# Start of a fused attention and mixture kernel: one batch of x loaded and normalised alone, weights behind it, inverse roots on GpSimd, identity products in TensorE's pauses

## The chip, the cores and the metric

One core of one Trainium2 chip runs the whole program in one launch. The metric is the device time of a run in microseconds. Engines are named TensorE (PE, and PEld for its weight loads), VectorE (DVE), ScalarE (ACT), GpSimd (POOL) and SyncE (SP, which issues most loads and stores).

## The reference

Inputs: x of 16 batches x 128 tokens x 256 features, a context of 16 x 128 x 128, and positions of two coordinates per token. All of it is float32.

```python
x = x + xattn(layernorm(x), ctx, pos)      # 32 heads of 8, axial rotation of q and k
x = x + ffn(layernorm(x))                  # shared part + 6 of 32 experts per token

def layernorm(x): return (x - mean(x)) / sqrt(var(x) + 1e-5)

def xattn(x, ctx, pos):
    q = rope(x @ Wq, pos)
    k, v = split(ctx @ Wkv); k = rope(k, pos)
    return softmax(q k^T / sqrt(8)) v @ Wout + bout
```

The second half is a mixture of experts with grouped top-6 routing. The change does not touch it.

## The kernel before, in words

The program has two blocks, `attention` (from line 175) and `mixture` (from line 687). Each writes one instruction stream per engine, with semaphores between them, in an order laid down by hand. A stream runs in program order, so an instruction that waits holds all that stands behind it on its engine. The block of attention ends with all its engines before the mixture begins.

Attention works batch by batch (128 tokens). `periods` (line 242) calls `period(b)` for b = -3 to 17. In period b the kernel works on batch b's exponentials and weighted values, on batch b+1's logits, on batch b+2's keys and on batch b+3's normalised input and projections. Each period has eight slots g. So b = -3 holds only the input of batch 0, b = -2 that of batch 1 with the key transposes of batch 0, and b = -1 has the first logits.

What stands in the start, by engine:

- SyncE issues all loads on one queue, in this order (lines 284 to 292): positions, x batches 0 to 3 (512 KB), the first context (64 KB), WQ, WKV, WO (256 KB each), the broadcast bias BO (128 KB), then x batches 4 to 7, 8 to 11 and 12 to 15. `period` adds the further contexts, the four copies that spread kT into kz (line 305, one batch at a time, after `kT_ok` and `kz_zero`), and the rows of negated maxima (line 312).
- GpSimd fills constants: identities `identf` and `identh` (lines 323 to 328), zeros and ones of `tokst` and `V`. Then it waits for BO and, per batch, adds BO to x once its normalised copy exists (`add_bias`, line 341), and for every batch but the first makes `split` (line 258): the rotated q and k are summed and cut into a high and a low f16 part. In b = -3 it fills both kz with zeros (line 352).
- ScalarE takes the sine (line 361), the square root of variance + epsilon for batches 0 to 3 (`std`, line 363) and, in b = -1, for batches 4 to 15 (line 408). `norm` (line 368) makes xn, the normalised batch, from scale rs1 and bias nb1. `evac_xcT` copies the transposed xn and context out of PSUM, and lines 404 and 420 copy the transposed q (qst) and k (kT).
- VectorE makes the angles, then `statistics(0, 4, 0)` (line 445): four bn_stats, four bn_aggr, plus epsilon, then the rotation tables, the reciprocal of ScalarE's root, and nb1 = -mean * rs1. Per batch it rotates with `rope_cos` (line 475) and `rope_sin` (line 482). It makes the split of batch 0 (line 544). `statistics(4, 16, 1)` (line 546) follows the rotation of batch 1. The maxima of the logits are `row_max` (line 490).
- TensorE waits for WQ, WKV and WO together (line 646). Per batch come `transpose_xc` (line 556), `project_k`, `project_q` (lines 564, 568), then transposes of k and q, `project_v`, `logits_q`, `logits_k`, `weigh_values` and the output steps. `transpose_xc` of a batch waits until the rotation of the batch before has read the bank M1 (`rope_ok`).

## Time and profile before

| what | us |
|---|---|
| runs (three) | 378.28, 380.01, 381.38 |
| median of the runs | 380.01 |
| the profiled execution's own time | 381.89 |
| its span, first to last instruction | 380.1 |
| attention block, from the start | to about 221.6 |
| TensorE, VectorE, ScalarE, GpSimd busy | 323.4, 231.2, 200.1, 153.4 |

The rows below are from one profiled execution. Times count from the start of the span. In a timeline row, the first number is the start, the second the time until the last of the merged instructions ends, and the bracket tells how long the engine stood idle before and what ended that. DVE is VectorE, ACT ScalarE, POOL GpSimd; "q" behind a name is the engine's instruction sequencer, which issues loads. PEclk is the TensorE clock that the throttle granted, as a share of full speed.

### The profile page before, as it was taken

What the parts mean: (1) busy time and instruction counts of PE and PEld (TensorE: products, weight loads), DVE (VectorE), ACT (ScalarE), POOL (GpSimd) and SP (SyncE); (2) the same over time, 40 slices, a digit from 0 to 9 for tenths busy, and PEclk for the clock granted to TensorE, in tenths of its full rate; (3) what the DMA queues carried; (4) which work ended last, traced back from release to release, by engine and by line L of the source; (5) the groups of instructions that cost most, each with busy time, mean ns of one, the idle gap of its engine ahead of it and who ended that gap; (6) DMA issues with size and microseconds to landing.
All of it is one profiled execution on the core that took longest, in us unless ns stands there. A gap on an engine that the chain in (4) does not pass through costs nothing. (4 is left out here: it accounts for less than half of the span.)

```text
span 380.1 us, 9475 instructions
## 1 busy us (share of the span) xinstructions
PE 323.4 (85%) x3094; PEld 218.2 (57%) x3094; DVE 231.2 (61%) x650; ACT 200.1 (53%) x390; POOL 153.4 (40%) x240
## 2 busy tenths in 40 slices
PE   0776998999999999999979738797999989999940
PEld 0455676777777777777656423445574765555520
DVE  4486777767777767777757444588757242544430
ACT  3236766767677776776766457382324341333310
POOL 4555431455324554235400065035498520425560
PEclk9999999999999999999998956999999998999995
DMA  6411113444444454443310013302214174974446
GB/s 173 167 35 37 30 29 111 128 120 109 129 125 122 111 139 109 132 113 100 96 45 0 2 37 130 118 0 44 72 35 148 31 226 119 290 211 50 51 48 221
DMA packets 33293, 37.93 MB, mean 100 GB/s; under 512 B 7808, under 2 KB 27568, under 8 KB 33200
## 3 DMA queue, kind: packets, MB, share of 16 engines
q1 hardware_dynamic: 22610, 22.03, 19.9%
q10 hardware_dynamic: 8030, 11.93, 11.1%
q0 software_dynamic: 2624, 3.61, 5.7%
q8 instruction: 16, 0.26, 0.3%
q14 instruction: 13, 0.11, 0.1%
HBM read 26.36 MB, written 8.96 MB: 93 GB/s over the span
## 5 line engine op out<-in xcount | busy, mean ns | idle before, releaser
L494 DVE TENSOR_REDUCE mx<-bank 128x4 f16<-128x512 f32 x128 | 88.1, 689 | 29.7 <-PE bank L599 28.4
L391 ACT ACTIVATE pw<-bank 128x512 f32<-128x512 f32 x128 | 76.8, 604 | 36.3 <-PE bank L623 21.1
L264 POOL TENSOR_TENSOR rot<-t 128x256 f32<-128x256 f32 x30 | 21.2, 726 | 95.4 <-DVE t L487 95.4
L599 PE MATMUL bank<-kz,qst 128*128 128x512 f16 x128 | 48.8, 382 | 4.0 <-issue 2.9
L612 PE MATMUL bank<-qst,kz 128*128 128x128 f16 x512 | 50.3, 221 | 0.7 <-DMA qst<-mxs 0.7
L612 PEld LDWEIGHTS bank<-qst,kz 128*128 128x128 f16 x512 | 35.8, 98 | 15.2 <-issue 6.7
L623 PE MATMUL bank<-pw,V 128*32 128x128 f32 x1024 | 38.6, 280 | 0.0
L931 POOL DMA_INDIRECT acc<-ac,dst x16 | 23.6, 1472 | 36.9 <-ACT ac L1013 24.7
L623 PEld LDWEIGHTS bank<-pw,V 128*32 128x32 f32 x1024 | 25.4, 110 | 13.5 <-issue 12.6
L1233 PE MATMUL mbank<-hT,WSG 128*128 128x512 f16 (+1 forms) x144 | 32.0, 379 | 0.0
L501 DVE COPY mxs<-bank 8x128 f16<-8x128 f16 x64 | 13.3, 208 | 19.9 <-PE bank L603 19.9
L1233 PEld LDWEIGHTS mbank<-hT,WSG 128*128 128x128 f16 (+1 forms) x144 | 15.1, 106 | 15.5 <-ACT ac L967 0.4
L1245 PE MATMUL mbank<-WSD,ac 128*128 128x256 f32 (+1 forms) x96 | 21.7, 382 | 2.0 <-POOL ac L887 2.0
L887 POOL TENSOR_TENSOR ac<-ac,sg 128x512 f32<-128x512 f32 (+1 forms) x9 | 11.8, 1323 | 25.5 <-ACT ac L967 25.4
L275 POOL TENSOR_TENSOR tokst<-rot,tokst 128x256 f16<-128x256 f32 x30 | 20.2, 673 | 4.4
L1017 ACT ACTIVATE ac<-mbank 128x176 f32<-128x176 f32 x16 | 5.1, 318 | 31.2 <-PE mbank L1323 29.4
L1323 PE MATMUL mbank<-ring_gu,xbT 128*64 128x352 f32 x112 | 20.5, 488 | 0.8 <-ACT xbT L807 0.8
L1245 PEld LDWEIGHTS mbank<-WSD,ac 128*128 128x128 f32 (+1 forms) x96 | 18.0, 190 | 5.5 <-POOL ac L887 3.0
L420 ACT COPY kT<-bank 128x1024 f16<-128x1024 f16 x16 | 16.2, 1011 | 7.8 <-PE bank L584 6.6
L603 PE MATMUL bank<-identh,mx 128*128 128x128 f16 x64 | 14.3, 223 | 5.9 <-DVE mx L494 4.5
L570 PE MATMUL bank<-WQ,xcT 128*128 128x256 f32 x64 | 18.6, 418 | 0.0
L643 PE MATMUL bank<-WO,attnT 128*128 128x256 f32 x64 | 17.5, 398 | 0.5 <-ACT attnT L387 0.5
(189 smaller groups left out, 627.1 us busy)
## 6 DMA issues: line engine op xcount, KB each, us to landing
ring_gu<-in_L_ffn_w_gate_up ACTq DMA_DIRECT2D x20, 352.0 KB
kz<-kT SPq DMA_DIRECT2D x64, 64.0 KB, 2.0
ring_dn<-in_L_ffn_w_down ACTq DMA_DIRECT2D x10, 352.0 KB
ring_gu<-in_L_ffn_w_gate_up SPq DMA_DIRECT2D x8, 352.0 KB
X<-in_x SPq DMA_DIRECT2D x4, 512.0 KB, 7.6
table<-ac SPq DMA_DIRECT2D x8, 256.0 KB, 2.1
acc<-X SPq DMA_DIRECT2D x4, 512.0 KB, 3.1
out<-acc SPq DMA_DIRECT2D x4, 512.0 KB, 5.3
```

The source lines that it names most:

```text
L264: eng.tensor_tensor(rot[:, part], t1[:, part], t2[:, part], ALU.add).then_inc(rot_ok[w], 1)
L275: eng.tensor_tensor(tokst[m.par][:, w, :, a:a + HD], r, hi, ALU.subtract)
L391: act.activation(pw[g % 4][:, :], STB[g % 2][:, :], ACT.Exp, scale=SCALE).then_inc(exp_ok, 1)
L494: dve.tensor_reduce(mx[u // 2 % 2][:, u % 2:8:2], SB[u % 2][:, :].rearrange("p (j t) -> p j t", j=4), axis=AX.X, op=ALU.max, negate=True). ...
L570: ins = pe.matmul(M1[:, 0:D], xcT[m.par][:, c, :], WQ[:, c, :], start=(c == 0), stop=(c == DK - 1))
L599: pe.matmul(SB[u % 2][:, :], qst[m.par][:, u, :], kz[m.par][:, :, u, :], start=True, stop=True).then_inc(s_mm, 1)
L612: ins = pe.matmul(STB[g % 2][:, j * P:j * P + P], kz[m.par][:, j, g, :], qst[m.par][:, g, :], start=True, stop=True)
L623: ins = pe.matmul(OB[m.par][32 * j:32 * j + 32, (g % 4) * P:(g % 4) * P + P], V[m.par][:, a:a + SLOT], pw[g % 4][:, j * P:j * P + P], star ...
L931: pool.indirect_dma_start(acc[:, :], bass.IndirectOffsetOnAxis(ap=dst[0:USED, k:k + 1], axis=0), ys[j][0:USED, :], None, compute_op=ALU.ad ...
L1233: ins = pe.matmul(GU[2 * (i % 2) + w][0:n, :], WSG[:, c, u, w * SHARED + a:w * SHARED + a + n], hT[:, v, c, 512 * k:512 * k + 512], start= ...
L1245: ins = pe.matmul(DN[m % 2][:, 0:D], ac[k % 2][0:n, f, j * P:j * P + P], WSD[0:n, f, :], start=(f == 0), stop=(f == 2))
L1323: ins = pe.matmul(EB[k % 2][lane, 0:2 * INNER], xbT[:, c, e * CAP:e * CAP + LANE], ring.gu[place][:, e % 2, c, :], start=(c == 0), stop=(c ...
```

## The change

- `XPART` cuts x into loads of batch 0 alone, batches 1 to 5, 6 to 10 and 11 to 15. Behind batch 0 and the first context come WKV and WQ; BO and WO go behind all of x.
- TensorE waits for WKV and WQ only, after its first transposes. WO shares the semaphore of BO, which GpSimd's first bias and TensorE's first output projection wait for.
- The statistics are taken for batch 0, for 1 to 3 and for 4 to 15. `factors` (nb1 = -mean * rs1) is a step of its own. That for batches 1 to 3 stands behind the rotation of batch 0.
- rs1 is (variance + epsilon) to the power -0.5, one tensor_tensor on GpSimd (`spread`), where ScalarE took a square root and VectorE a reciprocal.
- GpSimd fills kz after the power for batches 1 to 3 and before it waits for BO. The power for batches 4 to 15 stands in b = -1, ahead of that period's bias and split.
- `keep_warm(n)` issues n f16 products of the identity with 256 columns into the bank OB[1], whose result nobody reads: 30 before the first transposes, 4 behind them, 12 behind project_q of batch 0, 6 behind that of batch 1.

```diff
@@ -35,6 +35,7 @@
 NB, D, DC = 16, 256, 128
 NH, HD = 32, 8
 QUADS, SLOT = NH // 4, 32
+XPART = [0, 1, 6, 11, NB]
 DK = D // P
 MAXROW = 3 * HD
 HALF = SLOT // 2
@@ -206,6 +207,7 @@
         st1 = sb("st1", [P, NB, 6])
         mv1 = sb("mv1", [P, NB, 2])
         rs1 = sb("rs1", [P, NB, 1])
+        power = sb("power", [P, NB])
         nb1 = sb("nb1", [P, NB, 1])
         ang = sb("ang", [P, 2, NB, 2, 2])
         turns = sb("turns", [P, 2, NB, 2, 2])
@@ -222,7 +224,7 @@
         ctx_in_s = [sem(f"ctx_in{i}") for i in range(2)]
         consts, consts2, kz_zero = sem("consts"), sem("consts2"), sem("kz_zero")
         mx_zero = sem("mx_zero")
-        stat1, mv1_ok, std1, rs1_ok = sem("stat1"), sem("mv1_ok"), sem("std1"), sem("rs1_ok")
+        stat1, mv1_ok, rs1_ok = sem("stat1"), sem("mv1_ok"), sem("rs1_ok")
         turn_s, sin_s, rope_tab = sem("turn_s"), sem("sin_s"), sem("rope_tab")
         xn_ok, x_biased = sem("xn_ok"), sem("x_biased")
         xcT_mm, xcT_ok = sem("xcT_mm"), sem("xcT_ok")
@@ -283,13 +285,14 @@
         def _(sp):
             sp.dma_start(POS[:, :, :], pos.rearrange("b p a -> p b a")).then_inc(pos_in, 16)
             for c in range(4):
-                sp.dma_start(X[:, 4 * c:4 * c + 4, :], xr[:, 4 * c:4 * c + 4, :]).then_inc(x_in[c], 16)
+                part = slice(XPART[c], XPART[c + 1])
+                sp.dma_start(X[:, part, :], xr[:, part, :]).then_inc(x_in[c], 16)
                 if c == 0:
                     sp.dma_start(CT[0][:, :], ctx_in[0]).then_inc(ctx_in_s[0], 16)
+                    sp.dma_start(WKV[:, :], wkv).then_inc(w_in, 16)
                     sp.dma_start(WQ[:, :, :], wq.rearrange("(c p) n -> p c n", p=P)).then_inc(w_in, 16)
-                    sp.dma_start(WKV[:, :], wkv).then_inc(w_in, 16)
-                    sp.dma_start(WO[:, :, :], wout.rearrange("(c p) n -> p c n", p=P)).then_inc(w_in, 16)
-                    sp.dma_start(BO[:, :], bout.rearrange("(a n) -> a n", a=1).broadcast_to([P, D])).then_inc(bo_in, 16)
+            sp.dma_start(BO[:, :], bout.rearrange("(a n) -> a n", a=1).broadcast_to([P, D])).then_inc(bo_in, 16)
+            sp.dma_start(WO[:, :, :], wout.rearrange("(c p) n -> p c n", p=P)).then_inc(bo_in, 16)
 
             def period(b):
                 m1, m4 = b + 1, b + 4
@@ -342,14 +345,25 @@
                 at_least(pool, xn_ok, m.n + 1)
                 pool.tensor_tensor(X[:, m.n, :], X[:, m.n, :], BO[:, :], ALU.add).then_inc(x_biased, 1)
 
-            pool.wait_ge(bo_in, 16)
+            pool.memset(power[:, :], -0.5).then_inc(consts, 1)
+            pool.wait_ge(consts, 7)
+
+            def spread(a, e, k):
+                pool.wait_ge(mv1_ok, k + 1)
+                pool.tensor_tensor(rs1[:, a:e, 0], nb1[:, a:e, 0], power[:, a:e], ALU.pow).then_inc(rs1_ok, 1)
+
+            spread(0, 1, 0)
+            spread(1, 4, 1)
+            pool.wait_ge(xn_ok, 1)
+            for i in range(2):
+                pool.memset(kz[i][:, :, :, :].rearrange("p j q t -> p (j q t)").bitcast(F32), 0.0).then_inc(kz_zero, 1)
+            pool.wait_ge(bo_in, 32)
 
             def period(b):
+                if isinstance(b.n, int) and b.n == -1:
+                    spread(4, NB, 2)
                 if inside(b + 3):
                     add_bias(b + 3)
-                    if isinstance(b.n, int) and b.n == -3:
-                        for i in range(2):
-                            pool.memset(kz[i][:, :, :, :].rearrange("p j q t -> p (j q t)").bitcast(F32), 0.0).then_inc(kz_zero, 1)
                     if not (isinstance(b.n, int) and b.n == -3):
                         split(pool, b + 3)
             periods(pool, period)
@@ -360,13 +374,8 @@
             act.wait_ge(turn_s, 5)
             act.activation(ang[:, :, :, :, :], turns[:, :, :, :, :], ACT.Sin, scale=TWO_PI).then_inc(sin_s, 1)
 
-            def std(a, e, k):
-                act.wait_ge(mv1_ok, 2 * k + 2)
-                act.activation(rs1[:, a:e, 0], nb1[:, a:e, 0], ACT.Sqrt).then_inc(std1, 1)
-            std(0, 4, 0)
-
             def norm(m):
-                act.wait_ge(rs1_ok, 2 if isinstance(m.n, int) and m.n < 4 else 4)
+                act.wait_ge(rs1_ok, 6 if not isinstance(m.n, int) or m.n > 3 else 4 if m.n else 2)
                 at_least(act, xcT_mm, m.n)
                 act.activation(xn[:, :], X[:, m.n, :], ACT.Identity, bias=nb1[:, m.n, :],
                                scale=rs1[:, m.n, :]).then_inc(xn_ok, 1)
@@ -391,7 +400,7 @@
                         act.activation(pw[g % 4][:, :], STB[g % 2][:, :], ACT.Exp, scale=SCALE).then_inc(exp_ok, 1)
                     if g == 0 and inside(m1):
                         at_least(act, v_mm, m1.n + 1)
-                        act.wait_ge(consts, 6)
+                        act.wait_ge(consts, 7)
                         at_least(act, pv_mm, QUADS * b.n)
                         act.copy(Vh[m1.par][:, :, :, 0:HD], M0[:, 0:D].rearrange("p (f h d) -> p f h d", f=2, d=HD)).then_inc(v_ok, 1)
                     if g == 0 and inside(m3):
@@ -404,8 +413,6 @@
                             act.copy(qst[m1.par][:, :, :], M0[:, :].bitcast(F16).rearrange("p (q t) -> p q t", q=QUADS)).then_inc(qst_ok, 1)
                     if g == 4 and inside(m4):
                         norm(m4)
-                    if g == 4 and isinstance(b.n, int) and b.n == -1:
-                        std(4, NB, 1)
 
                     if g in (1, 4, 6) and not isinstance(b.n, int):
                         ring.load_first(act, b.n - 2, (1, 4, 6).index(g))
@@ -445,30 +452,30 @@
             def statistics(a, e, k):
 
                 for j in range(a, e):
-                    if j % 4 == 0:
-                        dve.wait_ge(x_in[j // 4], 16)
+                    if j in XPART:
+                        dve.wait_ge(x_in[XPART.index(j)], 16)
                     dve.bn_stats(st1[:, j, :], X[:, j, :]).then_inc(stat1, 1)
                 for j in range(a, e):
-                    dve.wait_ge(stat1, j + 1)
+                    dve.wait_ge(stat1, j + k + 1)
                     ins = dve.bn_aggr(mv1[:, j, :], st1[:, j, :])
-                ins.then_inc(mv1_ok, 1)
-                dve.wait_ge(mv1_ok, 2 * k + 1)
+                ins.then_inc(stat1, 1)
+                dve.wait_ge(stat1, e + k + 1)
                 dve.tensor_scalar(nb1[:, a:e, 0], mv1[:, a:e, 1], EPS, None, ALU.add).then_inc(mv1_ok, 1)
-                if k == 0:
-
-                    dve.wait_ge(sin_s, 1)
-                    sin = ang[:, 0].rearrange("p b a f -> p b (a f)")
-                    cos = ang[:, 1].rearrange("p b a f -> p b (a f)")
-                    for r in range(2):
-                        dve.tensor_copy(RC[:, :, :, r], cos)
-                        dve.tensor_scalar(RS[:, :, :, r], sin, -1.0 if r == 0 else 1.0, None, ALU.mult).then_inc(rope_tab, 1)
-                dve.wait_ge(std1, k + 1)
-                dve.reciprocal(rs1[:, a:e, 0], rs1[:, a:e, 0]).then_inc(rs1_ok, 1)
+
+            def factors(a, e, k):
                 dve.wait_ge(rs1_ok, 2 * k + 1)
                 dve.scalar_tensor_tensor(out=nb1[:, a:e, 0], in0=mv1[:, a:e, 0], scalar=-1.0, in1=rs1[:, a:e, 0],
                                          op0=ALU.mult, op1=ALU.mult).then_inc(rs1_ok, 1)
 
-            statistics(0, 4, 0)
+            statistics(0, 1, 0)
+            factors(0, 1, 0)
+            dve.wait_ge(sin_s, 1)
+            sin = ang[:, 0].rearrange("p b a f -> p b (a f)")
+            cos = ang[:, 1].rearrange("p b a f -> p b (a f)")
+            for r in range(2):
+                dve.tensor_copy(RC[:, :, :, r], cos)
+                dve.tensor_scalar(RS[:, :, :, r], sin, -1.0 if r == 0 else 1.0, None, ALU.mult).then_inc(rope_tab, 1)
+            statistics(1, 4, 1)
             dve.wait_ge(mx_zero, 2)
             dve.wait_ge(rope_tab, 3)
 
@@ -541,9 +548,11 @@
                     if g == 6 and inside(m3):
                         rope_sin(m3)
                     if g == 6 and isinstance(b.n, int) and b.n == -3:
+                        factors(1, 4, 1)
                         split(dve, m3)
                     if g == 6 and isinstance(b.n, int) and b.n == -2:
-                        statistics(4, NB, 1)
+                        statistics(4, NB, 2)
+                        factors(4, NB, 2)
                     if g == 7 and isinstance(b.n, int) and b.n == 15:
                         ahead.split_lo(dve, raw_wsg)
             periods(dve, period)
@@ -639,11 +648,18 @@
 
             def project_out(m):
                 pe.wait_ge(attnT_ok, m.n + 1)
+                if isinstance(m.n, int) and m.n == 0:
+                    pe.wait_ge(bo_in, 32)
                 for c in range(DK):
                     ins = pe.matmul(OB[m.par][:, 0:D], attnT[:, c, :], WO[:, c, :], start=(c == 0), stop=(c == DK - 1))
                 ins.then_inc(wo_mm, 1)
 
-            pe.wait_ge(w_in, 48)
+            def keep_warm(n):
+
+                for i in range(n):
+                    pe.matmul(OB[1][:, 0:2 * P], identh[:, :], identf[:, :].bitcast(F16), start=True, stop=True)
+
+            keep_warm(30)
 
             def period(b):
                 m1, m2, m3, o = b + 1, b + 2, b + 3, b + -1
@@ -667,12 +683,17 @@
                             weigh_values(b, q)
                     if g == 0 and inside(m3):
                         transpose_xc(m3)
+                        if isinstance(b.n, int) and b.n == -3:
+                            keep_warm(4)
+                            pe.wait_ge(w_in, 32)
                     if g == 1 and inside(m1):
                         transpose_q(m1)
                     if g == 1 and inside(m3):
                         project_k(m3)
                     if g == 2 and inside(m3):
                         project_q(m3)
+                        if isinstance(b.n, int) and b.n < -1:
+                            keep_warm(12 if b.n == -3 else 6)
                     if g == 3 and inside(o):
                         transpose_outputs(o)
                     if g == 5 and inside(o):
```

## Rows read from the trace of the kernel before

**Rows 1.** Stretch (from:to, us, busy us of PE, PEld, DVE, ACT, POOL, PEclk, DMA share, GB/s)

```profile
0.00:21.70 21.70, 8.46 (x26) 5.65 (x26) 10.18 (x39) 6.65 (x10) 10.14 (x22) 1.00 0.51 149
```

**Rows 2.** Timeline of all engines, first batch

```profile
5.91 1.41 DVE L450 BATCH_NORM_STATS2 st<-X 128x6 f32<-128x256 f32 x4 [0.29 <-DMA X<-in_x]
...
5.98 1.28 ACT L365 ACT_TABLE_LOAD   x1
...
7.63 0.17 DVE L456 TENSOR_SCALAR nb<-mv 128x4 f32<-128x4 f32 x1
...
8.31 0.16 DVE L468 SCALAR_TENSOR_TENSOR nb<-mv,rs 128x4 f32<-128x4 f32 x1
...
8.51 0.60 ACT L371 ACTIVATE xn<-X,nb,rs 128x256 f32<-128x256 f32 x1 [0.47 <-DVE nb L468]
...
9.37 0.66 PE L561 MATMUL bank<-identf,xn 128*128 128x128 f32 x2 [9.37 <-DMA WO<-in_L_xattn_Wout]
```

**Rows 3.** Load of WO: issue (timeline), size and us to landing; a later stretch

```profile
4.03 0.43 SPq L291 DMA_DIRECT2D WO<-in_L_xattn_Wout  x1
...
WO<-in_L_xattn_Wout SPq DMA_DIRECT2D x1, 256.0 KB, 5.2
...
14.00:15.00 1.00, 0.00 (x0) 0.00 (x0) 1.00 (x3) 0.00 (x0) 1.00 (x2) 1.00 0.32 97
```

**Rows 4.** Timeline of TensorE

```profile
10.81 1.22 PE L566 MATMUL bank<-WKV,xcT 128*128 128x256 f32 x2 [0.57 <-ACT xcT L377]
...
19.54 1.06 PE L584 MATMUL bank<-identh,tokst 128*128 128x128 f16 x8
...
23.48 1.01 PE L577 MATMUL bank<-identh,tokst 128*128 128x128 f16 x8
...
24.28 1.17 PE L566 MATMUL bank<-WKV,xcT 128*128 128x256 f32 x2
...
26.54 0.59 PE L599 MATMUL bank<-kz,qst 128*128 128x512 f16 x2
...
28.91 0.23 PE L603 MATMUL bank<-identh,mx 128*128 128x128 f16 x1 [1.78 <-DVE mx L494]
...
29.20 0.61 PE L584 MATMUL bank<-identh,tokst 128*128 128x128 f16 x8
```

**Rows 5.** Timeline of VectorE

```profile
13.88 0.69 DVE L480 TENSOR_TENSOR t<-bank,RC 128x512 f32<-128x512 f32 x1 [5.40 <-PE bank L570]
...
14.49 0.74 DVE L487 TENSOR_TENSOR t<-bank,RS 128x256 f32<-128x256 f32 x2
...
21.06 4.01 DVE L450 BATCH_NORM_STATS2 st<-X 128x6 f32<-128x256 f32 x12
...
25.91 0.44 DVE L456 TENSOR_SCALAR nb<-mv 128x12 f32<-128x12 f32 x1
...
26.98 0.69 DVE L494 TENSOR_REDUCE mx<-bank 128x4 f16<-128x512 f32 x1
```

**Rows 6.** Timeline: kT, the second batch on GpSimd, the kz loads

```profile
20.64 1.01 ACT L420 COPY kT<-bank 128x1024 f16<-128x1024 f16 x1 [3.37 <-PE bank L584]
...
21.22 1.41 POOL L264 TENSOR_TENSOR rot<-t 128x256 f32<-128x256 f32 x2 [5.53 <-DVE t L487]
...
21.73 2.53 SPq L305 DMA_DIRECT2D kz<-kT  x4
...
25.59 0.73 POOL L343 TENSOR_TENSOR X<-X,BO 128x256 f32<-128x256 f32 x1
```

**Rows 7.** GpSimd: three rows of the timeline, one group of the page

```profile
0.31 0.10 POOL L1384 MEMSET const-float32-0.0<- 128x1 f32 x1 [0.31 <-issue]
...
1.66 0.28 POOL L327 TENSOR_SCALAR_AFFINE_SELECT identh<-identh 128x128 f16<-128x128 f16 x1
...
11.46 3.54 POOL L352 MEMSET kz<- 128x2048 f32 x2
...
L931 POOL DMA_INDIRECT acc<-ac,dst x16 | 23.6, 1472 | 36.9 <-ACT ac L1013 24.7
```

## The prediction

> **What bounds the kernel now.** I read the start first, because every edit acts in the first 30 us. The stretch [rows 1] shows a TensorE that is busy 8.46 of the first 21.7 us, VectorE 10.18 and the loads half of it. Nothing is saturated there; it is one chain of waits through five engines, and the wait that ends last at each joint is the thing to read. After 30 us the attention loop repeats the same order per batch, and none of its waits is tied to the clock on the wall, so I let a shift of its start pass unchanged to the end. The chain of waits that the profile follows back from the last instruction stops at the joint between attention and mixture, so it says nothing of the start: I followed the start in the timelines.
>
> The first joint is the first normalised batch [rows 2]. VectorE is free from 5.62 (5.91 less its idle 0.29), waits for a load of four batches, takes 1.41 us for four statistics and has added epsilon at 7.80. After ScalarE's root, VectorE's reciprocal and the bias product, the norm starts at 8.51 and ends at 9.11. TensorE starts at 9.37. Its releaser is the load of WO, issued at 4.03 and landed 5.2 us later, at 9.2 [rows 3]; that load just overtakes the data, and removing it alone would give about 0.1 to 0.2.
>
> The second joint is TensorE's own speed [rows 4]. The granted clock is written as 1.00 in this stretch [rows 1], yet eight f16 products of 128 columns take 1.06 us at 19.54 and 0.61 at 29.20. Eight at 23.48 are 0.80 from the next group at 24.28, 0.10 each, and the fast group is shorter by 0.45, so 0.05 each: the levels 1.2 and 2.4 GHz. Everything up to the group at 24.28 (two products of 256 columns in 1.17) runs at the lower one. By the timeline TensorE works nearly unbroken from 21.7 until it rises, at about 25. The pause of 1.78 us before 28.91 did not undo it: the next group at 29.20 is a fast one.
>
> The third joint is VectorE [rows 5]. After the second rotation it takes the statistics of twelve batches, 21.06 to 26.35, waits for the root, and is free for the first maximum at 26.98. The first two logits products run from 26.54, 0.59 for both, so VectorE is late by a few tenths at most; the kz loads, issued from 21.73 behind kT [rows 6], would release the logits not much before 26.3. These two branches meet at 26.98, and what I forecast is when they meet afterwards.
>
> **The change, step by step.**
>
> *First statistics.* One batch in place of four. The work from 5.91 to 7.80 is 1.89; three fewer statistics at 0.333 ((1.41-0.41)/3) and three fewer aggregates at about 0.065 leave 0.69. The load of 128 KB in place of 512 KB should be in before VectorE is free at 5.62, as the 512 KB were at 5.91. So epsilon is added at 5.65+0.69 = 6.34 in place of 7.80.
>
> *Inverse root on GpSimd.* Gone are the root, the reciprocal and one load of ScalarE's function table; the second table load ran beside VectorE's statistics, so it is worth nothing here. New are two hand-overs at about 0.1 and the power itself, d1 for one column, d12 for twelve. No row shows a power. From below the nearest is GpSimd's fill of 128x1 at 0.10; from above its dearest short kind of instruction, the indirect DMA issue at 1.47 [rows 7]. An addition of 256 columns takes 0.73 [rows 6], so plain elements are cheap; a power is not a plain element. I take 0.4 for one column, nearer to the fill, and 0.9 for twelve, nearer to the top since it has twelve times the work. The norm of batch 0 starts at 6.34+0.1+0.4+0.07+0.16+0.04 = 7.1, in place of 8.51.
>
> The Trainium skill, GPSIMD Engine Reference, section Performance versus the Vector engine, puts elementwise work there at about half of VectorE's speed and advises against it. By that, doubling a VectorE step of about 0.2 for each, the two powers would be 0.8 together in place of my 1.3, and the result by this estimate 0.5 us better. No row here shows whether a power is such work.
>
> *Identity products.* GpSimd has both identities at 1.66+0.28 = 1.94 [rows 7], so thirty products of 256 columns run from 2.0. At the lower level one is about 0.21 (twice 0.10, rounded up for a tail), 6.4 in all, end 8.4. If the clock rises about as late behind the first of them as it did behind 21.7, at 6 at the latest, nineteen are slow and eleven take 0.11: end 7.3. xn is ready at 7.1+0.6+0.1 = 7.8. So the fast case costs nothing and the slow one 0.6. The four after the transposes run beside ScalarE's copy of about half a us (0.45 fast, 0.85 slow), and the twelve after the first projection end 1.3 later, in the time in which VectorE rotates: covered. The six after the second projection stand directly ahead of the transposes of k: 0.65 on the path, nothing covers them.
>
> *First projections.* From the transposes' start to that of project_k it was 1.44 (9.37 to 10.81), of which the transposes are about 0.9 and ScalarE's copy the rest; with fast transposes it is 1.1, so project_k starts at 8.9 in place of 10.81. The loads: only WKV and WQ are waited for, 720 KB with all that is ahead of them (16+128+64+256+256), where 1360 KB (16+512+64+3x256) had landed at 9.2: no wait. k, q and the tail took 3.07 until the rotation at 13.88 [rows 4, 5]; fast it is 1.6. Rotation starts at 10.5; it takes 1.35 [rows 5] and ends at 11.85 in place of 15.23: 3.4 gained so far.
>
> *Batch 1.* Its bias product now stands behind the rotation of batch 0 on VectorE. Before, its xn lay ready. Now 0.2 on VectorE, 0.6 norm, 0.2 hand-overs: transposes at 12.85, so about 0.85 of wait is new. What queues behind the instruction is the split of batch 0, later by 0.2 and covered. Statistics of batches 1 to 3 want the second load (640 KB, 1360 KB in all with those ahead, so about 9.2 or earlier) and end by 10.7; if later, they push the rotation one for one. Then project_k(1) 1.1 later at 13.95, its two projections at 1.36 (3.07 less a tail of 0.35, halved), and transposes of k at 13.95+1.36+0.65 = 15.95 in place of 19.54, kT at 16.6 in place of 20.64 [rows 6]: 4.0 gained on the kz branch. GpSimd's two fills of kz (3.54 together [rows 7]) now start behind the power of three columns, about 11.3, and end about 14.9, ahead of kT's end at 17.6.
>
> *Twelve statistics.* Second rotation starts at 13.95+1.6 = 15.55, ends 16.9, where the statistics began at 21.06. They take 5.2 (21.06 to 26.35) and end at 22.1. Then 0.1+0.9+0.07+0.17: VectorE is free at 23.3. Before it was 26.98. This branch gains 3.7, the other 4.0; the later one counts: **3.7 us**.
>
> *Queues.* BO and WO are now last on SP's queue. All start loads are in by about 15 (the stretch 14 to 15 moves 97 GB/s, the tail [rows 3]), and the bytes are the same. GpSimd waits for both before its first bias: two of 0.73 [rows 6], free at 16.5; the second batch's split is wanted at 17.0. Its 4.4 (21.22 to 25.59) end at 21.4, and the twelve-column power behind it is wanted at 22.2. Cost zero, with a margin of 0.5 at the split and 0.8 at the power. The first output projection wants WO tens of us later.
>
> **Sum.** Profiled run 381.89, its span 380.1; minus 3.7 gives 378.2 and 376.4. The median of the runs is 380.01, where I apply the same 3.7: **376.3 us**. Both powers at 0.1 would add 1.1, but the kz branch caps the gain near 4.4 (its 4.0 and the 0.4 by which the logits were ahead): 375.6. Both at 1.47 take 1.6 off: 377.9.
>
> **Rivals.**
> (A) As above, chance 0.62. Own range 375.2 to 378.2: the two bounds, and a little for the runs, which lie from 378.28 to 381.38.
> (B) *The power is dear, slower than before.* If GpSimd handles it lane by lane, it costs c per column, and d1+d12 is 13c+0.2. The branch has room of 5.0 for both (3.7+1.3), so it decides from c = 0.37 us; at c = 0.8 it is 10.6, and the time 380.0+5.6 = 385.6. VectorE stands waiting for the twelve columns, with the first maximum behind it. For it: no row of a power. Against: all GpSimd rows seen are under 3 ns a column. Chance 0.11. The Trainium skill (GPSIMD Engine Reference, section Instruction dispatch) adds a start-up of about 6 us for the first call of freshly loaded code, which would make the time by an estimate 381.9; the first addition at 0.73, like the later ones, shows no such thing, for a resident kind.
> (C) *The clock does not rise or falls back.* All fast terms go back to slow ones: first products end 8.4, project_k(0) waits for the four extra (10.1), the twelve extra hold the transposes to 15.5, the six cost 1.3, transposes of k end about 22.05 against 20.60, and the gain turns into a loss of about 1.1: 381.1. For it: TensorE idles about 1.3 us before batch 1. Against: the pause of 1.78 us. A case half way to mine gives 378.7. Chance 0.12. [...]
> (D) *Bias and WO late.* GpSimd holds split and power until they land. From a landing at 16.3 on, VectorE's wait grows one for one: at 17.5 the time is 377.5. Against it, the bytes are no more than before. Chance 0.15, with other small losses of that size among it.
>
> **How the numbers follow.** A 1% difference (3.8 us, limit 376.2) is about what a measurement can tell from none. A lies on the limit: of its 0.62 I give 0.32 to a gain over 1% and 0.30 to within 1%. D stays within 1%, and so does C but for 0.01; B gives 0.08 to slower by over 1% and 0.03 to within 1%. Faster 0.32, within 1% 0.59, slower 0.09. The range leaves out B above its first third, most of C's worst, and a little below: 375.0 to 379.3.
>
> **What would show it.** In the changed profile: norm of batch 0 near 7.1; q products of batch 0 at half length; xn(1) behind the rotation; kT near 16.6; the twelve-column power and its length; the first maximum near 23.3 with VectorE, not kz, ahead of it; after it, the same distances as before. Wrong if a power row exceeds 2 us, if q's products stay at 0.63, if the split of batch 1 waits for a load, or if the first maximum moves by 3.7 and the end does not.

## The result: slower by 0.6%, where 1% faster was forecast

Median of the changed kernel 381.12 us (21 runs), of the kernel before 378.46 (21 runs). The ratio is 1.0062, with a 95% interval of 1.0037 to 1.0087: a loss of about 2.3 us (1.4 to 3.3), where I had forecast a gain of 3.7. The three runs known at the prediction had a median 1.5 above that of the 21.

The profiled executions alone would mislead: the span is 379.1 against 380.1 before. The loop of the profiled execution before happened to lose time that the other did not (an output projection 12.5 us behind the last at 205, with TensorE at a granted clock of 0.66 in that stretch; 10.0 us in the changed one). So I compare landmarks of the start: the first maximum, and the first output projection, which stood at 53.22 before and stands at 56.15 now. The first two rows are of the kernel before, the third of the changed one:

```profile
37.53 0.38 PE L599 MATMUL bank<-kz,qst 128*128 128x512 f16 x1 [1.68 <-issue]
...
53.22 1.03 PE L643 MATMUL bank<-WO,attnT 128*128 128x256 f32 x4
...
56.15 1.03 PE L654 MATMUL bank<-WO,attnT 128*128 128x256 f32 x4
```

The 53.22 holds a pause of TensorE of 1.68 us for which the profile shows no wait. In the other thirteen profiled executions the longest of this kind between 30 us and this landmark is 0.8. So a distance from the kernel before at the first output projection is 1.7 larger without that pause (the changed kernel: 2.9 as it stands, 4.6 without); distances between the other kernels are free of it. Only single executions are compared here in any case.

The timeline of the changed kernel, first 24 us, cut to the rows that are used (start us, us, engine line operation, count, what ended the idle time before it):

```profile
6.50 0.59 POOL L353 TENSOR_TENSOR rs<-nb,power 128x1 f32<-128x1 f32 x1 [0.76 <-DVE nb L463]
...
7.32 0.60 ACT L380 ACTIVATE xn<-X,nb,rs 128x256 f32<-128x256 f32 x1 [1.37 <-DVE nb L467]
...
10.65 1.08 DVE L457 BATCH_NORM_STATS2 st<-X 128x6 f32<-128x256 f32 x3 [2.96 <-DMA X<-in_x]
...
12.10 0.69 DVE L487 TENSOR_TENSOR t<-bank,RC 128x512 f32<-128x512 f32 x1
...
13.05 3.54 POOL L359 MEMSET kz<- 128x2048 f32 x2
...
13.55 0.60 ACT L380 ACTIVATE xn<-X,nb,rs 128x256 f32<-128x256 f32 x1 [4.52 <-DVE nb L467]
...
14.16 2.57 DVE L273 CAST tokst<-rot 128x256 f16<-128x256 f32 x1
...
15.60 0.66 PE L570 MATMUL bank<-identf,xn 128*128 128x128 f32 x2 [3.58 <-DMA CT<-in_ctx]
...
19.76 0.63 PE L660 MATMUL bank<-identf,identh 128*128 128x256 f16 x2
...
20.00 0.69 DVE L487 TENSOR_TENSOR t<-bank,RC 128x512 f32<-128x512 f32 x1 [0.88 <-PE bank L579]
...
21.04 0.73 PE L593 MATMUL bank<-identh,tokst 128*128 128x128 f16 x8
...
21.81 1.01 ACT L427 COPY kT<-bank 128x1024 f16<-128x1024 f16 x1 [4.33 <-PE bank L593]
```

Against [rows 2]: the norm of batch 0 starts at 7.32 in place of 8.51, as forecast (7.1). Against [rows 5]: the rotation starts at 12.10 in place of 13.88, so 1.8 of the gain is there. Then it goes. The norm of batch 1 is done at 14.15, but the transposes behind it start at 15.60, and each of them is slow again. The six identity products run from 19.76 up to the transposes of k, which begin at 21.04, where they began at 19.54 [rows 4].

What TensorE waited for in the first 32 us (total, times, longest):

```profile
PE bank L612 <- DVE mx L501: 3.7, 1, 3.7
...
PE bank L570 <- DMA CT<-in_ctx: 3.6, 1, 3.6
```

The second row is a wait that I did not have: the context of batch 1 is the load that ends last. The first row is the largest of all, and its source is in the timeline of the stretch that follows:

```profile
12.23 0.87 POOL L353 TENSOR_TENSOR rs<-nb,power 128x3 f32<-128x3 f32 x1 [5.15 <-DVE nb L463]
...
26.37 2.27 POOL L353 TENSOR_TENSOR rs<-nb,power 128x12 f32<-128x12 f32 x1 [0.53 <-DVE nb L463]
...
28.68 0.68 DVE L467 SCALAR_TENSOR_TENSOR nb<-mv,rs 128x12 f32<-128x12 f32 x1 [2.39 <-POOL rs L353]
...
29.29 0.68 DVE L501 TENSOR_REDUCE mx<-bank 128x4 f16<-128x512 f32 x1
...
31.22 0.23 PE L612 MATMUL bank<-identh,mx 128*128 128x128 f16 x1 [3.66 <-DVE mx L501]
...
31.50 1.02 PE L593 MATMUL bank<-identh,tokst 128*128 128x128 f16 x8
```

The power of twelve columns takes 2.27 us. VectorE stands for it, TensorE behind VectorE for 3.66, and after that pause the group of 31.50 takes 1.02, where its counterpart took 0.61 at 29.20 [rows 4]. In the stretch 31 to 38 the granted clock is 0.54 (the third number from the end of this row, whose columns are those of [rows 1]):

```profile
31.00:38.00 7.00, 5.99 (x34) 4.28 (x35) 4.35 (x11) 4.29 (x6) 3.29 (x7) 0.54 0.12 29
```

So the first maximum is 2.3 late against before (29.29 against 26.98), the first output projection 2.9 as the two executions stand.

### The profile page after: what moved, and what is told of

The parts are those of the page before. It is cut to its first block and busy times, and to the rows that moved or that the text cites. A ratio compares the mean times of both kernels' runs of the same rounds, so it can differ in the third digit from the quotient of the medians.

```text
span 379.1 us, 9582 instructions
## 1 busy us (share of the span) xinstructions
PE 328.5 (87%) x3146; PEld 222.5 (59%) x3146; DVE 234.3 (62%) x650; ACT 198.7 (52%) x387; POOL 157.4 (42%) x244
## 5 line engine op out<-in xcount | busy, mean ns | idle before, releaser
L1254 PEld LDWEIGHTS mbank<-hT,WSG 128*128 128x128 f16 (+1 forms) x144 | 15.1, 106 | 15.5 <-ACT ac L988 0.4
L427 ACT COPY kT<-bank 128x1024 f16<-128x1024 f16 x16 | 16.2, 1011 | 11.8 <-PE bank L593 10.6
L579 PE MATMUL bank<-WQ,xcT 128*128 128x256 f32 x64 | 17.3, 395 | 0.0
L413 ACT COPY qst<-bank 128x1024 f16<-128x1024 f16 x16 | 16.7, 1041 | 1.1 <-PE bank L586 1.1
```

Source lines behind the costliest of these rows:

```text
L579: ins = pe.matmul(M1[:, 0:D], xcT[m.par][:, c, :], WQ[:, c, :], start=(c == 0), stop=(c == DK - 1))
L1254: ins = pe.matmul(GU[2 * (i % 2) + w][0:n, :], WSG[:, c, u, w * SHARED + a:w * SHARED + a + n], hT[:, v, c, 512 * k:512 * k + 512], start= ...
```

## The experiments

Theory: two waits (the second context, the twelve-column power) and the clock that falls in the pauses they leave. Rivals: the identity products themselves, or something later in the loop. Each ratio is to the kernel before; each landmark is of one profiled execution.

| kernel | first maximum | eight transposes of k behind it | first output projection | granted clock between the two | ratio (95%) |
|---|---|---|---|---|---|
| before | 26.98 | 0.61 | 53.22 | 1.00 | 1 |
| changed | 29.29 | 1.02 | 56.15 | 0.87 | 1.0062 (1.0037 to 1.0087) |
| e1 context early | 29.38 | 1.06 | 56.66 | 0.82 | 1.0046 (1.0000 to 1.0092) |
| e2 twelve deferred | 27.81 | 0.61 | 52.72 | 1.00 | 1.0004 (0.9947 to 1.0061) |
| e3 no products | 28.42 | 1.06 | 56.22 | 0.84 | 1.0111 (1.0007 to 1.0214) |
| e4 kz filled early | 28.96 | 0.61 | 54.71 | 0.93 | 1.0096 (1.0047 to 1.0146) |
| e7 roots again | 24.91 | 0.61 | 51.80 | 0.87 | 0.9992 (0.9952 to 1.0032) |
| e5 = e1+e2+e4 | 24.08 | 0.61 | 49.71 | 0.93 | 0.9966 (0.9924 to 1.0009) |
| e8 e5, smaller load | 25.14 | 1.06 | 51.75 | 0.87 | 0.9972 (0.9929 to 1.0016) |
| e9 e8 without the six | 25.53 | 0.61 | 50.88 | 1.00 | 0.9960 (0.9920 to 0.9999) |
| e11 before + power | 28.92 | 1.06 | 56.39 | 0.82 | 1.0087 (1.0043 to 1.0130) |
| e12 pause filled | 28.96 | 0.61 | 54.76 | 0.93 | 1.0030 (0.9996 to 1.0064) |
| e13 before + products | 26.17 | 0.61 | 51.48 | 0.93 | 0.9988 (0.9951 to 1.0025) |
| e6 e5 without the six | 23.27 | 0.61 | 49.65 | 0.94 | 0.9928 (0.9895 to 0.9961) |

The third column tells the clock of that one group alone: in e4, e5, e6, e7, e12 and e13 it took 0.61, and the clock fell in the groups behind it, as the fifth column shows.

**e1, the second context early.** The later load of that context goes.

```diff
                 if c == 0:
-                    sp.dma_start(CT[0][:, :], ctx_in[0]).then_inc(ctx_in_s[0], 16)
+                    for i in range(2):
+                        sp.dma_start(CT[i][:, :], ctx_in[i]).then_inc(ctx_in_s[i], 16)
```

> Edit: the context of batch 1 is loaded right behind that of batch 0, ahead of the weights. Theory (the start is lost at three joints: the second context behind all loads, the power of twelve columns, and the clock that falls in the pauses that both leave): the transposes of batch 1 move from 15.6 to about 14.3 and are fast ones (0.4, not 0.66); then VectorE's split of batch 0, held up beside GpSimd's fill of kz until 19.1, is the late one, so the second rotation moves from 20.0 to about 19.2 only, the first maximum from 29.3 to about 28.5, the time about 1 us below the changed kernel. Rival (the identity products themselves are the loss): nothing behind the six products moves by more than 0.3, same time as the changed kernel.

Measured: the wait for the context is gone, but the second load of x landed only at 11.7 (10.65 in the changed kernel), so the rotation began at 13.16 and the second transposes at 15.27 and slow (0.69). A miss: I expected 14.3 and fast ones. The split of batch 0 then held the second rotation to 20.10, as the expectation had it. One link out of a chain of three gives nothing; first maximum and time are those of the changed kernel within what was measured.

**e2, the power's use deferred.** The power stays; only the instruction that waits for it moves.

```diff
                     if g == 6 and isinstance(b.n, int) and b.n == -2:
                         statistics(4, NB, 2)
-                        factors(4, NB, 2)
+                    if g == 7 and isinstance(b.n, int) and b.n == -1:
+                        factors(4, NB, 2)
```

> Edit: the bias product of batches 4 to 15, which waits for the twelve-column power, goes behind VectorE's work of the first logits (slot 7 of period -1). Theory: the power still takes 2.27 us, but the first maximum starts at about 27.3, behind the kz loads, in place of 29.3; TensorE's pause of 3.7 us shrinks below 2 and the slow stretch from 31 to 38 goes; first output projection at about 53.3 in place of 56.15; time 2.5 to 3 us below the changed kernel, level with the kernel before. Rival (the loss sits in the products, or later in the loop): the first output projection gains under 1 us and the time under 0.5.

```profile
26.20 2.28 POOL L353 TENSOR_TENSOR rs<-nb,power 128x12 f32<-128x12 f32 x1 [0.53 <-DVE nb L463]
...
27.81 0.69 DVE L501 TENSOR_REDUCE mx<-bank 128x4 f16<-128x512 f32 x1 [1.69 <-PE bank L609]
...
29.75 0.23 PE L613 MATMUL bank<-identh,mx 128*128 128x128 f16 x1 [1.77 <-DVE mx L501]
...
30.04 0.61 PE L594 MATMUL bank<-identh,tokst 128*128 128x128 f16 x8
```

The power is as long as before. TensorE's pause is 1.77, the group behind it is a fast one, the clock stays up to the first output projection, and that is at 52.72, 3.4 earlier than in the changed kernel. It is most of what the change had lost there (2.9 as it stands, 4.6 without the pause in the execution before). The time is level with before, as expected; its interval is wide and overlaps that of the changed kernel, so the landmarks carry this verdict.

**e3, no products.**

```diff
-            keep_warm(30)
...
-                            keep_warm(4)
...
-                            keep_warm(12 if b.n == -3 else 6)
```

> Edit: all identity products out. Theory: the first projections are slow again, the rotation of batch 0 ends about 0.4 later (12.5 in place of 12.1 as its start), the six products' 1.07 before the transposes of k go (kT at about 20.8 in place of 21.8), but VectorE's branch is the late one, so the first maximum stays within 0.5 of 29.3 and the time within 1 us of the changed kernel. Rival (the products are the loss): time 2 to 3 us below the changed kernel.

The first maximum came 0.9 earlier (the six were gone, and the second load of x landed at 9.40), a little more than I allowed. But TensorE then paused for 4.63 and the group behind was slow: the first output projection is at 56.22, and the time not below the changed kernel. The products are not the loss.

**e4, kz filled early.**

```diff
             spread(0, 1, 0)
-            spread(1, 4, 1)
-            pool.wait_ge(xn_ok, 1)
             for i in range(2):
                 pool.memset(kz[i][:, :, :, :].rearrange("p j q t -> p (j q t)").bitcast(F32), 0.0).then_inc(kz_zero, 1)
+            spread(1, 4, 1)
```

> Edit: GpSimd fills kz right behind the power of one column, ahead of the power of three. Theory: the fills run at about 7.1 to 10.7 beside an idle VectorE; VectorE's cast of 2.57 us in the split of batch 0 falls back to 0.28 and the split ends at about 16.5 in place of 19.1; nothing else moves, since the transposes of batch 1 wait for their context until 15.6: first maximum at 29.3, time within 0.5 of the changed kernel. Rival (the late split holds the second rotation back): first maximum earlier by over 0.5.

```profile
7.05 3.54 POOL L357 MEMSET kz<- 128x2048 f32 x2
...
14.23 0.28 DVE L273 CAST tokst<-rot 128x256 f16<-128x256 f32 x1
...
15.63 0.41 PE L569 MATMUL bank<-identf,xn 128*128 128x128 f32 x2 [3.60 <-DMA CT<-in_ctx]
...
30.90 0.23 PE L611 MATMUL bank<-identh,mx 128*128 128x128 f16 x1 [3.10 <-DVE mx L500]
```

The cast falls from 2.57 to 0.28, and the split of batch 0 is no longer the next thing in line. The transposes still wait for the context. The first maximum moved by 0.3 and the time did not show it: a hidden cost, as the theory had it. In this execution the clock was up for the group behind the pause of 3.10 (0.61), in contrast to that of 3.66, and down for the two products of 256 columns at 34.04 (1.06). The first output projection came at 54.71.

**e7, roots instead of powers,** in all three places (ScalarE's square root, VectorE's reciprocal).

```diff
+            def std(a, e, k):
+                act.wait_ge(mv1_ok, k + 1)
+                act.activation(rs1[:, a:e, 0], nb1[:, a:e, 0], ACT.Sqrt).then_inc(std1, 1)
...
-            spread(0, 1, 0)
-            spread(1, 4, 1)
...
-                    spread(4, NB, 2)
```

> Edit: the power goes, ScalarE's square root and VectorE's reciprocal come back in all three places (1, 3 and 12 batches); all else as changed. Theory (the twelve-column power of 2.27 us and the clock's fall behind it are the net loss): the norm of batch 0 is up to 0.7 later than 7.32, behind the second table load; the second context still holds the second transposes to 15.6; but the first maximum stands at about 27.3, as in e2, no slow stretch after 30, first output projection at about 53, time level with the kernel before and with e2. Rival (the loss is in the order of loads or the products): the time stays 2 us or more above the kernel before.

Level with before, as e2. The norm of batch 0 started at 7.90 in place of 7.32. The first maximum was 2.4 better than I expected: the second context let the transposes go at 15.05, the second projections ran fast (q's four products in 1.03, where they took 1.91 in the changed kernel), and the split was out of the way, since GpSimd, with no power to wait for, filled kz from 8.62 to 12.17. I had also expected no slow stretch after 30. There was one (granted clock 0.54 from 30 to 35), behind a pause of 2.28. So e7 changes more than the power, and a slow stretch behind the maxima does not need the power.

**e11, the power alone, added to the kernel before.** The opposite test: twelve columns by GpSimd, all else as before.

```diff
+                if isinstance(b.n, int) and b.n == -1:
+                    pool.wait_ge(mv1_ok, 4)
+                    pool.tensor_tensor(rs1[:, 4:NB, 0], nb1[:, 4:NB, 0], power[:, 4:NB], ALU.pow).then_inc(rs1_ok, 1)
...
-                    if g == 4 and isinstance(b.n, int) and b.n == -1:
-                        std(4, NB, 1)
```

> Edit: the kernel before with one part of the change alone: the inverse root of batches 4 to 15 as a power on GpSimd, at the place it has in the change. Theory: the power takes 2.27 us, the first maximum moves from 27.0 to 29.1 to 29.4, TensorE pauses for about 3.7 us ahead of the first transposed maximum and is slow behind it in most executions; first output projection 2.3 to 3.5 after that of before (53.22), time 2 to 3.5 us above the kernel before. Rival (the loss comes from the rest of the change): time within 1 us of the kernel before.

```profile
25.96 2.31 POOL L353 TENSOR_TENSOR rs<-nb,power 128x12 f32<-128x12 f32 x1 [0.53 <-DVE nb L460]
...
28.92 0.68 DVE L499 TENSOR_REDUCE mx<-bank 128x4 f16<-128x512 f32 x1
...
30.86 0.29 PE L608 MATMUL bank<-identh,mx 128*128 128x128 f16 x1 [4.22 <-DVE mx L499]
...
31.36 1.06 PE L589 MATMUL bank<-identh,tokst 128*128 128x128 f16 x8
```

The power alone makes the kernel before slower by 0.9% (0.4 to 1.3), 3.3 us, with a long pause and a slow group as in the changed kernel. The profiled execution is one of the longest of its twelve (385.4, their median 382.44), so the verdict rests on the ratio; the first maximum, 1.9 later, shows where. With e2 and e7 this carries the net loss: added alone it is there; with roots again (e7, whose interval ends at 1.0032, below the changed kernel's) it is gone, though other things moved there too; deferred (e2), most of it is gone from the landmarks.

**e12, the pause filled.** The changed kernel with 24 identity products behind the first two logits products.

```diff
+                    if g == 4 and isinstance(b.n, int) and b.n == -1:
+                        keep_warm(24)
```

> Edit: the changed kernel with 24 more identity products behind the first two logits products of period -1, in the pause in which all wait for the power. Theory: the first maximum stays at 29.3; TensorE is busy to about 30 and keeps the higher clock, the group of k's transposes behind it takes 0.61 and not 1.02; the first output projection is 0.7 to 1.5 earlier than 56.15 and the time about 1 us below the changed kernel: this is the clock's share of the loss. Rival (the clock falls whatever stands there, or costs nothing): first output projection within 0.3 of 56.15.

```profile
26.35 0.82 PE L660 MATMUL bank<-identf,identh 128*128 128x256 f16 x6
...
30.89 0.23 PE L612 MATMUL bank<-identh,mx 128*128 128x128 f16 x1 [1.75 <-DVE mx L501]
...
31.17 0.61 PE L593 MATMUL bank<-identh,tokst 128*128 128x128 f16 x8
...
34.03 1.06 PE L598 MATMUL bank<-WKV,xcT 128*128 128x256 f32 x2
```

The power still holds the maximum (28.96), but the group at 31.17 takes 0.61. The clock fell all the same, in the groups behind it: the row of 34.03 is at the lower level. e4, with nothing in its pause, went the same way (0.61, 1.06 at 34.04, clock 0.93, 54.71). So e12 does not show that the fill keeps the clock up. What both show against the changed kernel is the price of a longer slow stretch: the maximum is 0.33 earlier and the first output projection 1.4, so roughly 1.1 us go with the clock (0.93 against 0.87), by single executions. The ratio fell from 1.0062 to 1.0030; the intervals overlap, so the time alone does not show it.

**e13, the products alone, added to the kernel before** (30, 4, 12 and 6).

> Edit: the kernel before with the identity products alone (30 ahead of the wait for the weights, then 4, 12 and 6). Theory: the first transposes stay at 9.4, now fast; the first projections end 1.4 earlier and the rotation of batch 0 begins at 12.1 to 12.3 in place of 13.88; the second context, landed by about 14.5 to 15, then sets the second transposes (15.4 before); the six cost 0.65 to 1.3; kT at 19.5 to 20.8 in place of 20.64; first maximum 26 to 27; time within 1.5 us of the kernel before, rather below. Rival (the products are what loses 2 us): first maximum at 28 or later.

First maximum 0.8 earlier, first output projection 1.7 earlier (as much as the pause in the execution before), time 0.9988: no loss, and no gain that was measured.

**The way to a better version: e5, e8, e9, e6.** e5 joins the edits of e1, e2 and e4.

> Edits of e1, e2 and e4 together: second context early, twelve-column bias product deferred, kz filled early. Theory: none of the joints is left, so now the early start comes through: second transposes at 14.2 to 15.2 (set by the second load of x, 10.7 to 11.7 in the runs so far), k's transposes at about 17 to 18, first maximum at 23.5 to 25, first output projection at 49 to 51.5, time 2 to 3.5 us below the kernel before. Rival (a further wait in the start, such as BO and WO at the end of the queue, eats it): first maximum later than 26, time level with the kernel before.

The second transposes start at 14.70, the first maximum stands at 24.08, the first output projection at 49.71, all within what I expected. The time is 1.3 us below the kernel before (2.9 below to 0.3 above), less than the 2 to 3.5 that I had put, though the interval reaches into them; by itself it shows no gain.

e8 cuts the second load to three batches (`XPART = [0, 1, 4, 10, NB]`).

> Edit: e5 with the second load of x cut to batches 1 to 3 (384 in place of 640 KB); the later loads are six batches each. Theory: the second load lands about 1 us earlier, the rotation of batch 0 waits for the projection (10.7) and not for it, everything to the first maximum moves by 0.8 to 1.2 against e5, the time by about 1. Rival: VectorE's rotation isn't held by the load but by the projection; under 0.3.

It gave nothing (first maximum 25.14, 1.1 later than in e5: the clock fell within the second projections, q's four products taking 1.50 in place of 1.03). The first statistics of batch 1 began at 10.72 with no wait for a load in front of them: VectorE had been held to 10.6 by the fill of kz, which now runs beside its four small copies of the rotation tables. I had called VectorE idle there. The timeline of e6 has the same:

```profile
7.05 3.54 POOL L358 MEMSET kz<- 128x2048 f32 x2
...
7.21 3.44 DVE L476 COPY RC<-ang 128x64 f32<-128x64 f32 x1
...
10.80 1.08 DVE L457 BATCH_NORM_STATS2 st<-X 128x6 f32<-128x256 f32 x3
```

e9 is e8 without the six products behind the second projection.

> Edit: e8 without the six identity products behind the second projection. Theory: k's transposes start 0.65 earlier if the clock is up there (1.3 if it is down), the kz branch with them, first maximum 0.5 to 0.7 earlier than e8, if VectorE's statistics of twelve batches don't end later than the kz loads land; in that case 0. Rival (the six keep the clock up for what follows): the products after 25 us become slow and the first output projection is no earlier than in e8.

Its second transposes happened to be slow (0.69), so it does not separate the six; no verdict.

e6 is e5 without the six.

```diff
-                        if isinstance(b.n, int) and b.n < -1:
-                            keep_warm(12 if b.n == -3 else 6)
+                        if isinstance(b.n, int) and b.n == -3:
+                            keep_warm(12)
```

> Edit: e5 (second context early, twelve-column bias product deferred, kz filled early) without the six identity products, meant as the best version. Theory: k's transposes 0.65 to 1.3 earlier than in e5 if the clock is as in e5; first maximum at 23.4 to 25.5 depending on the clock at the second projections; first output projection at 49 to 51; time 2 to 3.5 us below the kernel before, so below both kernels. Rival (the six kept the clock up for the logits): first output projection later than 51.5 with slow products after 26 us.

```profile
14.36 0.44 PE L571 MATMUL bank<-identf,xn 128*128 128x128 f32 x2 [2.33 <-ACT xn L380]
...
16.87 0.61 PE L594 MATMUL bank<-identh,tokst 128*128 128x128 f16 x8
...
22.66 0.59 PE L609 MATMUL bank<-kz,qst 128*128 128x512 f16 x2 [0.87 <-DMA kz<-kT]
...
23.27 0.69 DVE L501 TENSOR_REDUCE mx<-bank 128x4 f16<-128x512 f32 x1
...
25.21 0.23 PE L613 MATMUL bank<-identh,mx 128*128 128x128 f16 x1 [1.95 <-DVE mx L501]
```

The second transposes wait for nothing but their norm, the transposes of k stand at 16.87 (15.95 in the prediction), the first maximum at 23.27. Ratio 0.9928 (0.9895 to 0.9961): 2.7 us (1.5 to 4.0) below the kernel before, and below the changed one. The first maximum is where I had forecast it for the change, 3.7 earlier than before, so the chain of sums holds once the waits that I had missed are gone. That such a shift passes unchanged to the end, which I took for granted, is within the interval and not shown. Whether leaving out the six is worth anything against e5 is not shown; the intervals overlap.

## Why the prediction was wrong, point by point

**First statistics, first norm: right.** 7.1 forecast, 7.32 measured; the power of one column 0.4 forecast, 0.59 measured.

**The steps that failed.** The first maximum came at 29.29, not 23.3, and one of my signs of being wrong came with it, a power row over 2 us. The 6.0 us split like this:

- *Batch 1*, the term for the second load of x ("so about 9.2 or earlier"): it landed at 10.65, and the rotation started at 12.10, not 10.5. 1.6 us. I had written "if later, they push the rotation one for one", and it did. Over the runs this load was in at 9.40 to 11.71; what moves it is open.
- *Batch 1*, its transposes: I named the bias product as what is new before the transposes (norm done at 14.15, as by my chain from the later rotation), but not the context of batch 1. It had landed at 15.2 before, just ahead of its use at 15.4, and lands at 15.5 now. A forecast that shifts everything by 2.5 us has to ask this of every load. 1.15 us, and with it a pause of 3.6 in which the clock fell.
- The clock behind that pause: from the second transposes to the rotation of batch 1, 2.7 forecast and 4.40 measured. 1.7 us. The row that I read (a pause of 1.78 that undid nothing) said nothing of one twice as long. In e2, e4 and e12 the transposes behind such a pause were still fast and the projections slow.
- *Twelve statistics*, term d12: 0.9 forecast, 2.27 measured, and the bias product 0.68 in place of 0.16. From the statistics' end to the maximum 3.0 in place of 1.2. 1.8 us. The three powers give a line: 0.59, 0.87, 2.27, so 0.44 + 0.15 per column. I had spread 1.3 over both by nearness to rows of other kinds, and my upper bound of 1.47 was itself too low.

The pieces sum to 6.25, less 0.25 by which the second rotation and the twelve statistics were shorter (I had also written 5.2 for 21.06 to 26.35, which is 5.29). By my own sum the two powers as measured, 2.86 together in place of 1.3, would still have left a gain of 2.1; the three pieces ahead of them had used it up. The net loss against before is then the power (from the statistics' end to the first maximum 3.0 where it had been 0.6) and some of the clock behind it, while what the early start gained was already gone at 21 us. How much of the net loss is the clock's is open: no run changes the clock alone.

**The rivals.** (B) had the place right and the price too high: c came out at 0.15, not 0.37, yet it decided, because the room of 5.0 that I gave it was not there. (C) I treated as a chance of its own, with the products to prevent it. In part it came true: the second projections ran slow and the clock fell behind the first maxima. Waits that I had missed made the pauses longer, but e5, e6 and e7 lost the clock behind the maxima after pauses of 1.77 to 2.28 there, and e12 lost it with the pause filled; what decides it is open. (D) did not happen: WO was in at about 15.3 (issued at 6.58, 8.7 to landing). GpSimd's first two biases ran from 16.56, behind the fills of kz, and ended at 18.18, 1.7 later than forecast (16.5), but the split behind them had its data only at 21.43.

**The price of a power.** Half of VectorE's speed for elementwise work on GpSimd (the Trainium skill, GPSIMD Engine Reference, section Performance versus the Vector engine) does not carry to a power: 0.59 and 2.27 stand against VectorE's reciprocals of 0.17 and 0.23. The start-up of about 6 us for a first call of freshly loaded code (the Trainium skill, same page, section Instruction dispatch) did not show: the first power fits the line of the later ones.

## What to carry to other kernels

When a chain is to start earlier, list every load and buffer that the steps behind it use, with its landing and its first use; those that were in by a few tenths are the next wait. An operation that no row shows deserves a test of its own length before it is put where an engine waits for it, and the instruction that waits is often easier to move than the operation is to speed up. A new wait on TensorE's path can be charged twice, when the clock falls behind it. And a landmark of one profiled execution can hold a pause of that execution alone: look through the stretch before you subtract it.

## What the runs showed of the hardware

- The power on GpSimd: 0.59 us for one column, 0.87 for three, 2.27 for twelve (128 partitions, float32), in every run within 0.05.
- A GpSimd instruction can hold one of VectorE until it ends. Next to the kz fill a cast from SBUF to SBUF took 2.57 in place of 0.28, and a copy of 64 columns 3.44 in place of 0.19 (e6), until the fill ended. Sums of two float32 SBUF tiles (0.76 for two at 13.49) and operations out of PSUM were not held. The Trainium skill, SBUF — State Buffer, section SBUF: two separate sides, has it as a lock that VectorE and GpSimd take for a whole instruction, for VectorE's operations in the fast two-port mode and for those with two SBUF inputs only against a GpSimd operation that reads SBUF. These rows agree: a fill reads nothing. So does the bias product of twelve columns, two inputs from SBUF: 0.68 where GpSimd's addition of 28.61 (0.72) started ahead of it, 0.17 at 26.89 in the kernel before, where GpSimd stood idle.
- TensorE's clock: the length of one pause does not tell whether the clock falls. Behind pauses of 3.24 to 4.63 us it was at 1.2 GHz in every case seen, at once or by the third group behind (e4 before the second transposes: pause 3.60, the two transposes 0.41, the products behind them 1.22 in place of 0.70 at the high level). After 3.10 in e4 and 1.75 in e12 eight transposes ran at 2.4 GHz (0.61), and the products at 34.04 and 34.03 at 1.2 GHz (1.06). Behind the same pause of 2.24 e9 was slow at once, e8 only within the fourth group (q's four products 1.50). Behind the same pause of 1.77 e2 and e9 kept the high level, e5 lost it at 27.92, behind a further pause of 0.79, and e8 at once. So the same program may well take either course; the landmarks of single executions scatter by that.
